# Five mixing products in one pass over stacked high and low parts, and the tanh product ahead of the last channel-mix product

## The reference, cut to what matters

```python
xa = _ln(x, ln1_w, ln1_b)
sx = concat([state, xa[:, :-1]]) - xa            # the token before, less the token
xxx = xa + sx * maa_x
t = tanh(xxx @ maa_w1).reshape(B, L, 5, 32)      # 512 -> 5 x 32
m = einsum('blfd,fdc->blfc', t, maa_w2)          # five mixing products, 32 -> 512 each
xw = xa + sx * (maa_w + mw)                      # and so xk, xv, xr, xg
# w from xw; r, k, v, g from xr, xk, xv, xg; then the recurrence over the tokens:
#   s = k v^T + w s,  out = r (u k v^T + s);  group norm, gate, Wo, residual
# channel mix: x = x + sigmoid(xr2 @ fWr.T) * (relu(xk2 @ fWk.T)^2 @ fWv.T)
```

## Time and profile before

| | |
|---|---|
| median of 3 runs | 4285.62 us |
| the profiled execution, its own time | 4279.43 us |
| its span | 4276.5 us |
| mean granted clock of TensorE | 0.955 |
| TensorE busy | 3728.2 us, 87% of the span |
| TensorE weight loads | 2870.8 us, 67% |
| VectorE busy | 2997.0 us, 70% |
| ScalarE busy | 2056.6 us, 48% |
| POOL busy | 1740.5 us, 41% |
| DMA queue of SP | 21.9% of 16 engines |

### The profile page before, as it was taken

One profiled execution on the slowest core, in us unless ns is written; L12 is line 12 of the kernel. 1 busy time (PEld: TensorE's weight loads), 2 busy tenths in 40 slices (PEclk: granted clock), 3 DMA queues, 4 the chain that ended last, 5 costly groups with the idle time before them and its releaser, 6 DMA issues. The chain is left out here.

```text
span 4276.5 us, 71639 instructions
## 1 busy us (share of the span) xinstructions
PE 3728.2 (87%) x21636; PEld 2870.8 (67%) x21636; DVE 2997.0 (70%) x6732; ACT 2056.6 (48%) x5384; POOL 1740.5 (41%) x1210
## 2 busy tenths in 40 slices
PE   5998898588888886999999778999999999999976
PEld 5777777467777765899999655666666666666643
DVE  5777777477777774655655338878787877888872
ACT  4777777466767674545545422333333333333322
POOL 2444444234344341000000125666666666666652
PEclk9999999699999997999999888999999999999987
DMA  3434434244444434001001110000000000000000
GB/s 110 104 98 108 103 96 104 84 124 115 108 106 110 118 103 125 30 29 44 29 29 44 61 60 18 23 24 23 24 23 24 23 24 23 24 23 23 23 18 15
DMA packets 146611, 256.58 MB, mean 60 GB/s; under 512 B 27184, under 2 KB 32048, under 8 KB 145424
## 3 DMA queue, kind: packets, MB, share of 16 engines
q1 hardware_dynamic: 146448, 254.49, 21.9%
HBM read 107.62 MB, written 33.55 MB: 33 GB/s over the span
## 5 line engine op out<-in xcount | busy, mean ns | idle before, releaser
L1205 POOL TENSOR_TENSOR c_S<-c_S,c_rT 128x1024 f32<-128x1024 f32 x256 | 557.6, 2178 | 468.1 <-DVE c_S L1483 441.9
L1483 DVE TENSOR_TENSOR_SCAN c_S<-c_wT,c_s,c_vb 128x256 f32<-128x256 f32 x1024 | 708.8, 734 | 45.0 <-issue 2.7
L1478 DVE TENSOR_TENSOR c_vb<-c_kT,c_vb 128x512 f32<-128x512 f32 x512 | 352.2, 688 | 296.2 <-PE c_vb L1649 265.9
L348 POOL TENSOR_TENSOR x_prob<-x_prob,x_rsums 128x512 f32<-128x512 f32 x256 | 274.7, 1073 | 480.5 <-DVE x_rsums L510 480.5
L348 POOL TENSOR_TENSOR s_prob<-s_prob,s_rsums 128x512 f32<-128x512 f32 x256 | 274.7, 1073 | 442.0 <-DVE s_rsums L510 442.0
L1649 PE MATMUL c_vb<-c_vhl,c_spread 128*128 128x512 f32 x512 | 301.2, 598 | 73.1 <-DVE c_S L1483 60.1
L404 ACT ACTIVATE x_prob<-x_t,x_tmin 128x256 f32<-128x256 f32 x512 | 256.4, 502 | 220.5 <-DVE x_tmin L503 220.5
L404 ACT ACTIVATE s_prob<-s_t,s_tmin 128x256 f32<-128x256 f32 x512 | 256.4, 502 | 202.9 <-DVE s_tmin L503 202.9
L866 PE MATMUL b_ps<-b_ln_high,b_w_high 128*128 128x256 f32 x1024 | 290.5, 284 | 14.7 <-DVE b_ln_low L808 14.7
L867 PE MATMUL b_ps<-b_ln_low,b_w_high 128*128 128x256 f32 x1024 | 290.5, 284 | 0.0
L868 PE MATMUL b_ps<-b_ln_high,b_w_low 128*128 128x256 f32 x1024 | 290.4, 284 | 0.0
(11 more groups left out here) (266 smaller groups left out, 10548.7 us busy)
## 6 DMA issues: line engine op xcount, KB each, us to landing
s_stack<-s_parts_qk SPq DMA_DIRECT2D x384, 128.0 KB, 2.4
x_stack<-x_parts_qk SPq DMA_DIRECT2D x384, 128.0 KB, 2.4
s_x_in<-in_x SPq DMA_DIRECT2D x16, 512.0 KB, 3.6
s_xb<-in_x SPq DMA_DIRECT2D x16, 512.0 KB, 4.0
x<-s_x_out SPq DMA_DIRECT2D x16, 512.0 KB, 4.7
x_enc<-in_ctx SPq DMA_DIRECT2D x16, 512.0 KB, 4.4
x_x_in<-x SPq DMA_DIRECT2D x16, 512.0 KB, 3.7
x_xb<-x SPq DMA_DIRECT2D x16, 512.0 KB, 4.2
```

The costliest lines, as they stand in the source:

```text
L348: nc.gpsimd.tensor_tensor(prob[:, h % 4, :, :], prob[:, h % 4, :, :], rsums[:, h, :].unsqueeze(2).to_broadcast([P, TC, T]), ALU.mult).then ...
L1205: nc.gpsimd.tensor_tensor(S[:, n % 4, :, 0:T], S[:, n % 4, :, 0:T], rT[:, par, :, :], ALU.mult).then_inc(z_ready, 1)
L1478: nc.vector.tensor_tensor(pair(vb, i), pair(kT[:, par, :, :], i), pair(vb, i), ALU.mult)
L1483: op = nc.vector.tensor_tensor_scan(S[:, n % 4, c, 1:T + 1], wT[:, par, c, :], vb[:, c, :], s0[:, par, c, n:n + 1], ALU.mult, ALU.add)
```

## The change

The mixing products get one instruction each. tanh is split in a high and a low part; three places of 32 rows hold high, low, high of one product's tanh, and against them stand high, high, low of its weights; two rows of ones carry the high and low part of the constant. The stacking is done per batch by SP with 15 copies (`stack_t`). `t` and `kv1` swap places in `FILLS`. The weights are staged in the space of S, cast by ScalarE and subtracted from by VectorE at the start. The constants same_in, centre and perm go into b0. The semaphores of the weights are joined in three groups, and the halving of fWv moves from after the first pass to after the second.

```diff
-             13: (["xaT0", "xaT1"], ["rr0"]), 14: (["rr1"], ["kv0"]), 15: (["kv1"], ["t"])}
+             13: (["xaT0", "xaT1"], ["rr0"]), 14: (["rr1"], ["kv0"]), 15: (["t"], ["kv1"])}
...
-        tT = sb("tT", P, 2, T)
+        MIXROWS = 3 * DM + 2
+        tS = sb("tS", MIXROWS, NMIX, T, dtype=F32R)
...
+        t_low, t_high = b1[:, 0:2, :], b1[:, 2:4, :].bitcast(F32R)
...
-        mix2 = sb("mix2", P, NMIX, C)
+        mix2 = sb("mix2", MIXROWS, NMIX, C, dtype=F32R)
+        mix2_in = S[0:MIXROWS, :, :, :].rearrange("p b c n -> p (b c n)")[:, 0:NMIX * C]
...
                 load_weight("maa_w1")
-                sp.wait_ge(zeros_ready, 1)
-                for j in range(NMIX):
-                    place = DM * j if j < 3 else DM * (j - 3)
-                    sp.dma_start(mix2[place:place + DM, j, :],
-                                 d["maa_w2"][DM * j % P:DM * j % P + DM, DM * j // P, :]).then_inc(mix2_loaded, 16)
-                    at = COL_AT["maa_" + "wkvrg"[j]]
-                    ones = 3 * DM if j < 3 else 2 * DM
-                    for c in range(KC):
-                        sp.dma_start(mix2[ones:ones + 1, j, c * P:(c + 1) * P],
-                                     d["cols"][:, at + c:at + c + 1].rearrange("p o -> o p"),
-                                     allow_slow_non_contiguous=True).then_inc(mix2_loaded, 16)
+                staged = mix2_in.rearrange("p (j n) -> p j n", j=NMIX)
+                for place in range(3):
+                    for block, n in ((0, 4), (1, 1)):
+                        for j in range(4 * block, 4 * block + n):
+                            sp.dma_start(staged[DM * place:DM * place + DM, j, :],
+                                         d["maa_w2"][DM * j % P:DM * j % P + DM, block, :]).then_inc(mix2_loaded, 16)
+                at = COL_AT["maa_w"]
+                for row in (3 * DM, 3 * DM + 1):
+                    sp.dma_start(mix2_in[row:row + 1, :].rearrange("o (j n) -> o j n", n=P),
+                                 d["cols"][:, at:at + NMIX * KC].rearrange("p (o j) -> o j p", o=1),
+                                 allow_slow_non_contiguous=True).then_inc(mix2_loaded, 16)
...
+                def stack_t(b):
+
+                    sp.wait_ge(tl_ready, b + 1)
+                    for j in range(NMIX):
+                        rows = slice(DM * (j % 3), DM * (j % 3) + DM)
+                        for place, x in ((0, t_high.bitcast(F32)), (1, t_low), (2, t_high.bitcast(F32))):
+                            sp.dma_start(tS[DM * place:DM * place + DM, j, :].bitcast(F32),
+                                         x[rows, j // 3, :]).then_inc(t_stacked, 16)
...
                     if "front" in parts:
                         stack_v(k + 1, 1 - par)
+                    if "norm" in parts:
+                        stack_t(k + 2)
...
-                nc.gpsimd.memset(mix2[:, :, :], 0.0).then_inc(zeros_ready, 1)
-                nc.gpsimd.memset(tT[:, :, :], 1.0)
+                nc.gpsimd.memset(tS[3 * DM:MIXROWS, :, :].bitcast(F32), 1.0)
+                nc.gpsimd.drain()
...
                 op.then_inc(consts_ready, 1)
+                act.wait_ge(mix2_loaded, 16 * (3 * NMIX + 2))
+                nc.scalar.copy(mix2[:, :, :].rearrange("p j n -> p (j n)"), mix2_in).then_inc(mix2_high, 1)
...
-                        nc.scalar.activation(tT[0:3 * DM, 0, :], unit(name)[0:3 * DM, 0:T], ACT.Tanh)
-                        nc.scalar.activation(tT[0:2 * DM, 1, :], unit(name)[0:2 * DM, T:2 * T], ACT.Tanh).then_inc(done, 1)
+                        for i, rows in ((0, 3 * DM), (1, 2 * DM)):
+                            op = nc.scalar.activation(t_low[0:rows, i, :], channels(name)[0:rows, i, :], ACT.Tanh)
+                        op.then_inc(done, 1)
+                        nc.scalar.drain()
+                        for i, rows in ((0, 3 * DM), (1, 2 * DM)):
+                            op = nc.scalar.copy(t_high[0:rows, i, :], t_low[0:rows, i, :])
+                        op.then_inc(th_high, 1)
...
                     if isinstance(k, int) and k == -2:
                         late_weights()
+                    if isinstance(k, int) and k == -1:
+                        half_of_last()
...
+                dve.wait_ge(mix2_high, 1)
+                low = mix2[2 * DM:3 * DM + 1, :, :].rearrange("p j n -> p (j n)")
+                nc.vector.tensor_tensor(low, mix2_in[2 * DM:3 * DM + 1, :], low, ALU.subtract).then_inc(mix2_ready, 1)
                 dve.sem_inc(emptied["dve"], units.per["dve"])
...
                         take(k, FILLS[n][0], parts, par)
+                        if n == 15 and "norm" in parts:
+                            dve.wait_ge(th_high, k + 3)
+                            for i, rows in ((0, 3 * DM), (1, 2 * DM)):
+                                op = nc.vector.tensor_tensor(t_low[0:rows, i, :].bitcast(F32R), t_low[0:rows, i, :],
+                                                             t_high[0:rows, i, :], ALU.subtract)
+                            op.then_inc(tl_ready, 1)
...
                         if name == "mw0":
-                            pe.wait_ge(emptied["act"], units.emptied(k + 1, "t"))
-                            pe.wait_ge(mix2_loaded, 16 * NMIX * (KC + 1))
+                            pe.wait_ge(mix2_ready, 1)
+                            pe.wait_ge(t_stacked, 16 * 3 * NMIX * k + 2 * 16 * 3 * NMIX)
                         j = "wkvrg".index(what[1])
-                        rows = 3 * DM + 1 if j < 3 else 2 * DM + 1
                         for a in range(2):
                             c = 2 * i + a
-                            op = nc.tensor.matmul(u[:, a, :], mix2[0:rows, j, c * P:(c + 1) * P], tT[0:rows, j // 3, :],
+                            op = nc.tensor.matmul(u[:, a, :], mix2[:, j, c * P:(c + 1) * P], tS[:, j, :],
                                                   start=True, stop=True)
```

More of the change, by code:

```diff
@@ L990, in phase_c @@
         same_u = sb("same_u", P, KC, P)
-        same_in = sb("same_in", P, P)
-        centre = sb("centre", P, P)
-        perm = sb("perm", P, 2, P)
+        same_in, centre, perm = b0[:, 0, 0:P], b0[:, 0, P:2 * P], b0[:, 1:2, :].rearrange("p o (a n) -> p (o a) n", a=2)
         centred = sb("centred", P, 2, P)
-        mix2 = sb("mix2", P, NMIX, C)
+        mix2 = sb("mix2", MIXROWS, NMIX, C, dtype=F32R)
+        mix2_in = S[0:MIXROWS, :, :, :].rearrange("p b c n -> p (b c n)")[:, 0:NMIX * C]
         w = {**w, **{n: sb(n, P, *shape) for n, shape in WEIGHTS_C.items()}}
@@ L1000, in phase_c @@
         ps = ctx.enter_context(nc.psum_tensor("c_ps", [P, 4, 2 * T], F32))
-        weights_loaded = {n: sem(n + "_loaded") for n in WEIGHTS_C}
-        consts_loaded, mix2_loaded = sem("consts_loaded"), sem("mix2_loaded")
+        weights_loaded = {i: sem(f"weights_loaded_{i}") for i in set(WEIGHT_GROUP.values())}
+        consts_loaded, mix2_loaded, mix2_high, mix2_ready = (
+            sem("consts_loaded"), sem("mix2_loaded"), sem("mix2_high"), sem("mix2_ready"))
+        th_high, tl_ready, t_stacked = sem("t_high"), sem("t_low_ready"), sem("t_stacked")
         zeros_ready, consts_ready, centre_ready, centred_filled, centred_ready = (
@@ L1026, in phase_c, with group_loaded @@
         out_d = out.rearrange("b (c p) n -> b p c n", p=P)
+        def group_loaded(name):
+            return 16 * list(WEIGHT_GROUP.values()).count(WEIGHT_GROUP[name])
         def unit(name):
@@ L1229, in _ @@
                 act.wait_ge(consts_loaded, 16)
-                act.wait_ge(zeros_ready, 2)
+                act.wait_ge(zeros_ready, 1)
                 nc.scalar.copy(gather[:, 24:32], same_in[:, :].rearrange("p (h j) -> p h j", j=RS)[:, :, 0])
@@ L1247, in late_weights @@
                 def late_weights():
-                    act.wait_ge(weights_loaded["Wv"], 16)
+                    act.wait_ge(weights_loaded[WEIGHT_GROUP["Wv"]], group_loaded("Wv"))
                     staged = g2T[:, :, :, :].rearrange("p a (c b) n -> p (a c) (b n)", b=2)
@@ L1256, in late_weights, with half_of_last @@
                     op.then_inc(wv_ready, 1)
-                    act.wait_ge(weights_loaded["fWv"], 16)
+                def half_of_last():
+                    act.wait_ge(weights_loaded[WEIGHT_GROUP["fWv"]], group_loaded("fWv"))
                     nc.scalar.activation(flat(w["fWv"]), flat(w["fWv"]), ACT.Copy, scale=0.5).then_inc(fwv_ready, 1)
@@ L1525, in weights @@
                 def weights(name):
-                    if name not in loaded:
-                        loaded.add(name)
-                        pe.wait_ge(weights_loaded[name], 16)
+                    if WEIGHT_GROUP[name] not in loaded:
+                        loaded.add(WEIGHT_GROUP[name])
+                        pe.wait_ge(weights_loaded[WEIGHT_GROUP[name]], group_loaded(name))
                     return w[name]
@@ L1684 @@
              "fWr": (KC, C), "fWv": (KC, C)}
```

(2 more changed lines are left out.)

2 lines of the change are left out of this document (1 added, 1 removed).

## The result

The kernel after takes 4458.14 us (median of 4 runs, 4457.27 to 4464.08), the kernel before 4284.74 us in the same comparison (4 runs, 4277.04 to 4286.47). The ratio is 1.0413, with a 95% interval of 1.0395 to 1.0432: slower, and by 173 us instead of the 113 us forecast, at the upper edge of the range of 4330 to 4460 (the ratio on the 4285.62 us that the forecast started from would be 4462.6 us).

The account below looks back on a forecast made before the run. VectorE was taken to set the pace where the mixing products lie. 82 us over 14 batches (5.85 each), 9 for the first and 22 for the start gave 113 us more: 4399 us, range 4330 to 4460.

Parts of the forecast that it names:

- VectorE sets the pace: Both stretches of stage four with mixing products: VectorE is the limit, so shorter products gain only 0.35 us per batch.
- SP's cadence: Stacking copies per batch: SP issues 15, 0.64 us apart, 2.4 us to land, so VectorE's second step starts 5.2 us later.
- rival B: Copies nearly free to issue, mw0 does not wait, only the start's cost stays: 4297 to 4303 us; chance 0.06.
- lower bound: Stacking copies at 0.43 us per issue and 1.9 us to land: 1.8 us later per batch, 4323 us in all.
- VectorE's 0.8 us falls where TensorE sets the pace: nothing for it.: Two tanh subtractions per batch: about 0.8 us on VectorE, costing nothing as long as kv1 (3.6 us) covers it.
- the low part is done at 3369.2: Batch timeline: tanh's low part ready then, the fifteenth copy issued at 3378.2 and landed at 3380.6; mw0 waits 7.1 us.
- the rest becomes waiting of TensorE: Of 5.2 us per batch saved on TensorE only 0.35 us counts; the remainder turns into waiting.
- the swap at nothing: Exchange of t and kv1: kv1 moves back by 3.7 us, at no cost.
- The residual is first used in step 5: Reason given for the free swap: the later residual load is not needed until step 5 of the next batch.
- the start, 22 us forecast: Start of stage four: weight loading, cast, subtraction and first copies make it 22 us later (15 to 30).
- The clock behind mw's wait: TensorE at half clock after the wait for copies: 1 us per batch, bounds 0 and 4.
- Rival C: TensorE stays at 1.2 GHz for most of the stretch behind the wait: up to 4475 us, middle 4445; chance 0.16.

Follow-up runs that it names:

- e1: Kernel after, with the stacking copies issued for the first sequence only and read by all later ones; 4359.76 us.
- e2: Kernel after, with a semaphore for each mixing product's copies, issued in the order of use; 4351.72 us.
- e8: Kernel after, with copies for the first sequence only and every mixing product issued four times; 4348.74 us.
- e11: Kernel after, with a semaphore per product, POOL's multiplication behind VectorE's subtraction, and every mixing product issued four times; 4325.88 us, ratio 1.0103 to before.
- e4: Kernel after, with POOL's last-step multiplication held until VectorE has written the low part of tanh; 4439.25 us.
- e5: Kernel after, with the mixing products mv and mg issued four times each; 4433.22 us.
- e13: Kernel after, with first-sequence copies only, mixing products issued four times, POOL behind the subtraction, and the old order of t and kv1; 4327.96 us.
- e9: Kernel before, with four full-precision products that nothing reads added ahead of the channel mix's second key product; 4265.03 us, ratio 0.9970.
- e10: Kernel after, with the two rows of constants read from one contiguous row instead of 5,120 single elements; 4417.40 us.
- e3: Kernel after, with the cast and subtraction of the mixing weights moved from the start to behind the first pass; 4433.91 us.

## Why the prediction was wrong

It had the sign (0.88 for slower) and the chain. The size was off by half, and the sum shows where: a batch was to cost 5.85 us and cost 9.0, so that the fifteen distances grew by 128 us instead of 91, and the start was to cost 22 us and cost 39.4. Another 8.1 us are the stage's later beginning, for which the forecast had no term. From the last twelve batches, one cost after the other taken away:

| step | batch, us | worth, us | forecast, us |
|---|---|---|---|
| after | 114.74 | | |
| no copies (e1; e2 the same) | 108.91 | 5.8 | 5.2 |
| about as much TensorE work as before (e8) | 107.37 | 1.5 | 1.0 for the clock, -0.35 for the time saved |
| no clash with POOL (e11) | 106.62 | 0.75 | 0 |
| before | 105.75 | 0.9 | 0 |

The step from e8 to e11 also brings the copies back, with a semaphore per product (by e2 they cost nothing then). The parts are not independent: on the kernel after itself e4's mend is worth 1.2 us, and so is e5's. The last row, 0.9 us, stays open between the subtraction and the order of the last place (e13).

- **Right: VectorE sets the pace** in both stretches. With the mixing products at well under half their time, TensorE waits for VectorE instead (3.04 us ahead of y), and nothing was gained.
- **Right: SP's cadence.** 0.63 us per issue, against 0.64 forecast from the earlier trace rows; rival B, cheap issues, is out. The landing took 1.9 us in the median, not 2.4. The forecast's lower bound used 1.9 us too, but no row of before stood behind it.
- **Wrong: "VectorE's 0.8 us falls where TensorE sets the pace: nothing for it."** Its price was read from an instruction of stage three, where POOL is nearly idle. Here it runs beside POOL's multiplication, which starts as soon as the last scan ends, as it does in every step; so 2.71 us, and the copies start 2 us later. The step behind "the low part is done at 3369.2" failed. The earlier trace rows could not show it; the timelines of VectorE and POOL side by side could.
- **Wrong: "the rest becomes waiting of TensorE",** booked at nothing. The forecast charged the clock for the new wait only. The 5 us freed are waits as well and cost clock in the second stretch (12.65 us instead of 10.12), where 0.35 us were to be gained. e5, e8 and e9 show the mechanism from three sides. The section of the Trainium skill that the prediction quotes ("TensorE: Matmul & The Clock Gate", "HAM oscillation — how this bites in real kernels") tells of waits for a transfer before every tile; the rows show the low clock behind waits for VectorE too (0.50 from 3326 to 3328), and the prediction applied it to one of the two places.
- **Wrong: the swap at nothing.** "The residual is first used in step 5": true for the residual, but kv1's first reader is VectorE, right at the end of the batch. 1.5 us a batch alone; where the copies bind, the swap still gains 2.5.
- **Wrong: the start, 22 us forecast and 39.4 measured.** The single elements were priced at 19 ns each over 16 engines, 6 us. Counted from their first issue they had landed after 30.9 us; 28.6 us go with them (e10). The price per element failed. From 2450 to 2470 the kernel after reads:

```profile
2450.00:2470.00 20.00, 0.00 (x0) 0.00 (x0) 0.00 (x0) 0.00 (x0) 0.00 (x0) 0.50 1.22 2
```

A share of 1.22 of 16 engines over 20 us is 390 us of packet time (above 1 means that packets overlap), some 76 ns for each of the 5,120 elements, by estimate, where 19 were assumed. How many engines shared them the trace does not say.
- **The clock behind mw's wait**, 1.0 us: right. Rival C (clock down for most of the stretch, 4 us) did not come true there; its middle, 4445 us, was nearer to the result than the forecast was, but by luck: other causes made it up.
- The first three distances grew by 20 us together where the forecast had some 21 (9 for the first, 2 x 5.85).

## What to carry to other kernels

A saving on an engine that waits is not free of effect: here it lengthened TensorE's waits, and TensorE paid for them with its clock. Before pricing such a saving at nothing, look at the granted clock behind the waits that are there already. An instruction's duration is only good for the neighbours that it had when it was measured; for VectorE with two inputs in SBUF, look at what POOL does at that moment. And a consumer that needs three transfers should not wait for fifteen: one semaphore per group, in the order of use, gave back 5.8 of 9 us here.

## What was not expected of the hardware

- Two rows of 2,560 single four-byte elements were issued in 3.44 us (6.16 in e3) and landed at most 27 us later, and SP's next two, ordinary issues took 18.59 us (15.26 in e3). The same rows read contiguously: 0.59 us, landed within 2.3.
- VectorE's 256-column subtraction takes 0.39 to 0.42 us alone and 2.39 to 2.40 us when it starts just after a 2.2 us multiplication of POOL's, ending 0.3 us behind it.
- VectorE pauses 3.3 to 3.7 us at the end of each round of the loop (kernels before and after). How much of it is hidden depends on what stands just ahead of it, and it fits the even and odd batches of different lengths (105.8 and 109.3 us in e8).
- Four full-precision products that nothing reads made the kernel before 0.3% faster; the granted clock behind one wait rose from 0.60 to 1.00.
